# Second self attention: the last eight tiles' query, key and value products as three products of split factors

## The reference

```python
def _L1_attn_ref(x, ...):                       # x: (64, 32, 256), 16 heads, 16 wide, latent width 32
    qkv = x @ c_attn_w.T + c_attn_b
    q, k, v = jnp.split(qkv, 3, axis=2)         # into heads
    q_lat = q @ q2l_w.T + q2l_b
    k_lat = k @ kv2l_w.T + kv2l_b
    v_lat = v @ kv2l_w.T + kv2l_b
    q_lat = q_lat * cos + _rotate_half(q_lat) * sin
    k_lat = k_lat * cos + _rotate_half(k_lat) * sin
    q_for_k = q_lat @ wqk_w.T + wqk_b
    att = softmax(causal(q_for_k @ k_lat.T * L ** -0.5))
    y = (att @ v_lat) @ l2o_w.T + l2o_b
    return y @ cproj_w.T + cproj_b
...
x = x + _L1_attn_ref(_layernorm(x), ...)
x = x + tanh(((_layernorm(x) @ weight) @ aux1) @ aux2 + bias)
```

## Time and profile before

| | us |
|---|---|
| median of 3 runs | 2626.02 (2624.39 to 2628.48) |
| profiled execution | 2620.7 |
| its span, first to last instruction | 2618.9 |
| busy over the span: PE | 2439.4 (93%) |
| PEld | 1903.6 (73%) |
| DVE | 1696.1 (65%) |
| ACT | 1282.9 (49%) |
| POOL | 1475.7 (56%) |

### The profile page before, as it was taken

The page is one execution under the profiler, slowest core; times in us unless marked ns, Lnnn a source line. Parts: engine busy times, 40 slices in busy tenths (PEclk is TensorE's granted clock), DMA queues, the critical chain, the costliest instruction groups (busy, mean ns, idle before and its releaser), DMA issues. The chain is left out here.

```text
span 2618.9 us, 64377 instructions
## 1 busy us (share of the span) xinstructions
PE 2439.4 (93%) x24513; PEld 1903.6 (73%) x24513; DVE 1696.1 (65%) x3970; ACT 1282.9 (49%) x2972; POOL 1475.7 (56%) x1676
## 2 busy tenths in 40 slices
PE   6898999999999999998797999599999999998997
PEld 3457788888887878786465579478888888886665
DVE  5676868687868677774575844366556655653665
ACT  3565656565656565654342324254455445543443
POOL 6896767575767675764672245565456545332233
PEclk9999999999999999999897999799999999999998
DMA  4232212111111121110002459532234323210001
GB/s 166 113 140 79 61 36 50 34 46 39 41 40 46 34 50 34 46 32 8 30 5 94 142 165 314 185 119 76 67 95 103 75 68 94 71 45 15 3 4 35
DMA packets 223075, 190.04 MB, mean 73 GB/s; under 512 B 88705, under 2 KB 210514, under 8 KB 222770
## 3 DMA queue, kind: packets, MB, share of 16 engines
q1 hardware_dynamic: 206386, 151.19, 19.2%
q0 software_dynamic: 10080, 30.00, 4.5%
q10 hardware_dynamic: 6304, 4.72, 0.6%
HBM read 151.53 MB, written 34.31 MB: 71 GB/s over the span
## 5 line engine op out<-in xcount | busy, mean ns | idle before, releaser
L288 POOL TENSOR_TENSOR rk<-ss,neg_half 128x32 f32<-128x32 f32 x64 | 348.6, 5447 | 247.6 <-DVE ss L270 247.6
L1768 PE MATMUL banks<-rowsT,qk 128*128 128x257 f32 x1024 | 243.1, 380 | 0.9 <-ACT qk L1689 0.9
L321 ACT ACTIVATE ksq<-kT 128x512 f32<-128x512 f32 x256 | 161.1, 630 | 160.3 <-DVE kT L264 160.3
L264 DVE COPY kT<-banks 128x512 f32<-128x512 f32 x256 | 177.0, 692 | 60.7 <-PE banks L375 56.6
L375 PE MATMUL banks<-x_hi,wk_hi 128*128 128x256 f32 x1024 | 213.4, 289 | 1.1 <-DVE kT L264 1.0
L1768 PEld LDWEIGHTS banks<-rowsT,qk 128*128 128x128 f32 x1024 | 189.4, 190 | 27.5 <-ACT qk L1689 1.2
L375 PE MATMUL banks<-x_hi,wk_lo 128*128 128x256 f32 x1024 | 206.8, 284 | 0.0
L375 PE MATMUL banks<-x_lo,wk_hi 128*128 128x256 f32 x1024 | 205.6, 282 | 0.3 <-DVE x_lo L256 0.3
L1222 ACT ACTIVATE score<-score,ntop 128x289 f32<-128x289 f32 x256 | 135.4, 530 | 115.6 <-DVE ntop L1103 115.4
L1577 POOL DMA_INDIRECT parts<-scratch_expert,address x128 | 131.9, 1030 | 93.0 <-DVE residual L1475 45.9
L1606 POOL CAST r_hi<-diff 128x512 fp32r<-128x512 f32 x64 | 41.5, 648 | 249.9 <-PE banks L1794 249.1
(11 more groups left out here) (368 smaller groups left out, 6539.7 us busy)
## 6 DMA issues: line engine op xcount, KB each, us to landing
rowsT<-in_ctxT SPq DMA_DIRECT2D x64, 257.0 KB, 2.8
wgu<-in_expert_gu SPq DMA_DIRECT2D x64, 256.0 KB, 3.9
rows<-in_ctx SPq DMA_DIRECT2D x64, 256.0 KB, 3.2
raw<-in_ctx SPq DMA_DIRECT2D x61, 256.0 KB, 2.7
scratch_qT<-qT SPq DMA_DIRECT2D x16, 512.0 KB, 2.6
scratch_kT<-kT SPq DMA_DIRECT2D x16, 512.0 KB, 3.0
q<-scratch_qT SPq DMA_DIRECT2D x64, 128.0 KB
kT<-scratch_kT SPq DMA_DIRECT2D x64, 128.0 KB
```

The source lines that it names most:

```text
L264: nc.vector.tensor_copy(m.kT[:, k, 2 * i:2 * i + 2, 0:ROWS], banks[i % 2].rearrange("p (a r) -> p a r", a=2)).then_inc(s.kT, 1)
L288: nc.gpsimd.tensor_tensor(m.rk[:], m.ss[:], kit.neg_half[:, 0:KF * H], ALU.pow).then_inc(s.rk, 1)
L321: nc.scalar.activation(m.ksq[:, 2 * i:2 * i + 2, :], m.kT[:, k, 2 * i:2 * i + 2, 0:ROWS], ACT.Square).then_inc(s.ksq, 1)
L1768: mm = nc.tensor.matmul(score[h][:, c - h * HALF, 0:CTX], m.qk[:, f, j, c * BT:(c + 1) * BT, :].rearrange("p h q -> p (h q)"), m.rowsT[:, ...
```

## The change

In `sa1`, tiles 8 to 15 (`SPLIT` = 8): the transposed rows are written as a high part in fp32r (`x_hi`, by ScalarE, in place of `xlT`) and a low part (`x_lo`, a subtraction on VectorE out of the same bank). The weights are split once into `w_hi` (ScalarE copies) and `w_lo` (VectorE subtractions), in six pieces `CUTS` of 512, 512 and 256 columns for each half, one piece at the end of each of the steps -4 to 1. `product` then runs, after the bias, x_hi·w_hi, x_hi·w_lo and x_lo·w_hi for both halves: six fp32r products in place of two f32 ones. Tiles 0 to 7 and `sa0` keep theirs.

```diff
@@ buffers
+                            w_hi=([P, FC, QKV], F32R), w_lo=([P, FC, QKV], F32R), x_hi=([P, 2, FC, P], F32R), x_lo=([P, 2, FC, P], F32R))
+        SPLIT = 8 if rotary else NT
+        CUTS = [(f, slice(i * 512, min(i * 512 + 512, QKV))) for f in range(FC) for i in range(3)] if rotary else []
@@ VectorE
+                def weights_low(c):
+                    f, part = CUTS[c]
+                    dve.wait_ge(s.w_hi, c + 1)
+                    nc.vector.tensor_tensor(r.w_lo[:, f, part], w[:, f, part], r.w_hi[:, f, part].bitcast(F32), ALU.subtract).then_inc(s.w_lo, 1)
+
+                def rows_low(n):
+                    dve.wait_ge(s.xlT, n + 1)
+                    past(dve, s.qk_ps, (n - 1) * 2)
+                    past(dve, s.v_ps, n - 1)
+                    nc.vector.tensor_tensor(r.x_lo[:, n % 2].rearrange("p f t -> p (f t)"), kit.psum(0)[:, 0:D], r.x_hi[:, n % 2].rearrange("p f t -> p (f t)").bitcast(F32),
+                                            ALU.subtract).then_inc(s.x_lo, 1)
@@ VectorE, step
                     if has(3):
                         queries_keys(n + 3)
+                    if has(5) and n + 5 >= SPLIT:
+                        rows_low(n + 5)
                     if has(4):
                         if rotary:
                             cosines(n + 4)
                         else:
                             key_sums(n + 4)
+                    if rotary and 0 <= n + 4 < len(CUTS):
+                        weights_low(n + 4)
@@ ScalarE, rows_T
-                    nc.scalar.copy(m.xlT[:, n % 2].rearrange("p f t -> p (f t)"), kit.psum(0)[:, 0:D]).then_inc(s.xlT, 1)
+                    out = m.xlT if n < SPLIT else r.x_hi
+                    nc.scalar.copy(out[:, n % 2].rearrange("p f t -> p (f t)"), kit.psum(0)[:, 0:D]).then_inc(s.xlT, 1)
@@ ScalarE, step
                         inner(n + 4)
+                    if rotary and 0 <= n + 4 < len(CUTS):
+                        f, part = CUTS[n + 4]
+                        nc.scalar.copy(r.w_hi[:, f, part], w[:, f, part]).then_inc(s.w_hi, 1)
@@ TensorE
                     past(pe, s.xlT, n)
+                    past(pe, s.x_lo, n - SPLIT)
@@ TensorE, product
+                    if n >= SPLIT:
+                        for x, y in ((r.x_hi, r.w_hi), (r.x_hi, r.w_lo), (r.x_lo, r.w_hi)):
+                            for f in range(FC):
+                                mm = nc.tensor.matmul(out, x[:, n % 2, f, :], y[:, f, columns], start=False, stop=(x is r.x_lo and f == FC - 1))
+                        return mm
@@ TensorE, values
                     pe.wait_ge(s.xlT, n + 1)
+                    if n == SPLIT:
+                        pe.wait_ge(s.w_lo, len(CUTS))
+                    past(pe, s.x_lo, n - SPLIT + 1)
```

More of the change, by code:

```diff
@@ L2064, in self_attention @@
             r = kit.buffers(st, one=([P, P], BF16), causal=([P, HC, S], BF16),
-                            lat=([P, 2 * H, S], F32), turn=([P, 2 * H, S], F32), qrT=([P, 512], F32), qb=([P, 1], F32))
+                            lat=([P, 2 * H, S], F32), turn=([P, 2 * H, S], F32), qrT=([P, 512], F32), qb=([P, 1], F32),
+                            w_hi=([P, FC, QKV], F32R), w_lo=([P, FC, QKV], F32R), x_hi=([P, 2, FC, P], F32R), x_lo=([P, 2, FC, P], F32R))
             w = wm.w
@@ L2069, in self_attention @@
             w = wm.w
-        s = kit.sems(stage, "zero one masked gain qb xl xlT_ps xlT qk_ps v_ps sq raw v ss scaled rss lat cosed turned qk qT_ps kT_ps qrT qrT_ps qT kT s_ps "
+        s = kit.sems(stage, "zero one masked gain qb xl xlT_ps xlT qk_ps v_ps sq raw v ss scaled rss lat cosed turned qk qT_ps kT_ps qrT qrT_ps qT kT s_ps w_hi w_lo x_lo "
                      "top shift p mass rmass prob pT y_ps yT o_ps biased x_add passed")
```

## The result

The changed kernel takes 2635.2 us (median of 5), the kernel before beside it 2625.0: ratio 1.0046, 95% interval 1.0032 to 1.0059. It is 10 us slower where 0.4 was forecast, outside the range. The profiled execution took 2634.6, its span is 2631.6.

What follows compares the result with a forecast made beforehand. TensorE's order of work was taken to bound the step in the second self attention. Products -5.3, filling +5.7 and pauses 0 gave +0.4 us on the 2626.02 median: 2626.4 us, range 2621.0 to 2631.0.

Steps and rivals of the forecast that it cites:

- TensorE sets the step: Second self attention, tiles 8 to 15 projected: TensorE's order of work is the step's length; shortest step 10.84 us, then about 10.2.
- The products' price: Query and key banks 0.33 us shorter each, 5.3 us saved over eight tiles; the values' gain counted at nothing.
- The rows' low part: VectorE's subtraction of about 0.4 us per changed tile, ahead of the cosines, hidden in its wait for keys: costs nothing.
- The filling: Splitting the weights in steps -4 to 1: VectorE's subtractions meet GpSimd at SBUF and delay TensorE, 5.7 us together.
- The pauses in issue: TensorE's pauses in runs of small matmuls, over the eight steps: between -1.2 and +1.3 us, taken as 0.
- The tail: Attention of tiles 12 to 15 behind the last product: same instructions, so no change in time.
- The slower rival: Instruction supply bounds TensorE's step, longer pauses eat the products' gain, only the filling's 5.7 us is left: 2631.7; chance 0.10.
- point of decision: The slower rival decides once the pause of a step grows by 0.66 us, from 0.48 to 1.14.

Runs made afterwards that it cites:

- e_fill: The change with SPLIT = NT: weights split in six pieces but no tile uses them, all 16 keep f32 products; ratio 1.0034 to the kernel before.
- c_after: The changed kernel run again without an edit, on another chip; ratio 1.0036 to the kernel before.
- c_before: The kernel before run once more without an edit, as a control; ratio 0.9999.
- e_moved: The change with VectorE's low parts of the weights taken one step later, ahead of the cosines; ratio 1.0007 to the kernel before.
- e_one_input: The change with VectorE's weight subtractions replaced by same-size maxima with one SBUF input, low parts zero; ratio 1.0017 to the kernel before.
- m_mm128: e_moved with 64 one-column products (128 TensorE instructions) ahead of its first step; ratio 0.9983 to the kernel before, 2639.2 us against 2644.9.
- e_moved_2: e_moved run once more, unchanged; ratio 1.0001 to the kernel before, 2645.2 us against 2644.9.
- g_pad127: e_gain with 127 semaphore increments on TensorE ahead of the first step; ratio 1.0034 to the kernel before, stage 194.8 us.
- a_pad165: The change with 165 semaphore increments on TensorE ahead of the first step; ratio 1.0125 to the kernel before.
- b_mm128: The kernel before with 64 one-column products (128 TensorE instructions) ahead of the first step; ratio 1.0010 to the kernel before, 2648.3 us.
- e_gain: The change with split weights as constants set once, so no filling; ratio 1.0014 to the kernel before, stage 203.1 us.

## Why the prediction was wrong, point by point

- **TensorE sets the step**: right. Its floor came down to 10.2 us.
- **The products' price**: right. 1.61 us a bank for 1.93; forecast 0.33 less, measured 0.32. The values are shorter and the queries start no sooner: in the change the values' bias is at 2510.99 and the first product of the queries at 2512.00 (the record of their bias is missing), 1.01 us for 0.99 from bias to bias before. That they would wait for ScalarE's latents held.
- **The rows' low part**: right. No wait of TensorE for it in any profile, and in the change's VectorE waits for the keys' product in each of the eight changed steps.
- **The filling**: right in mechanism and in size. 5.5 us of TensorE's waits against 5.7; the subtraction at 1.37 against "about 1.4". Open: whether a pause behind one of these waits takes some of it up. In the change's first profile the pause of step 1 is gone and 3.3 us are lost; in e_fill and c_after the wait in step 1 is followed by the longest pause of the profile, and about 2 us more are lost than the waits hold.
- **The pauses in issue**: the step that failed. I put them between -1.2 and +1.3 us, took 0, and priced them by an average per step, from the first self attention. They are not an average. They stand where a block of instructions ends near the end of the mix, and the change moved these ends: among the eight steps, from 54 and 26 instructions ahead (steps 8 and 11) to 14 and 32 (7 and 10). The eight steps then have 8 x 10.21 = 81.7 us of work and 89.8 of length, 8.1 us of pause and slow clock, where before has 8 x 10.84 = 86.7 and 90.5, 3.8. That is +4.3 for the 0 taken, three times the upper end.
- **What a pause costs**: missing altogether. I counted pauses as idle time. In the change the clock goes to its lower level behind those of steps 7 and 10, and 1.63 and 1.36 us of pause become 3.2 and 3.1 us of step. In the kernel before, behind 1.74 us of pause, it stays at 1.00, so nothing in its trace showed it in the middle of this stage.
- **The tail**: wrong. "Same instructions, same time" is not so when their place in the blocks moves. The tail takes 31.6 us for 27.9, with a pause of 2.31 us at the output product of step 14 and the lower clock from there to the end of the stage. The pause is most of the 3.7 us; what the clock adds is not separated, since before runs its last 7 us at the lower level too, and c_before, all at 1.00, is only 0.6 us shorter. e_moved and e_one_input have this pause too, e_fill, in which TensorE's instructions are those of before, does not. TensorE in the change, then the busy times with the clock, from the change and from before:

```profile
2591.12 2.08 PE L2453 MATMUL banks<-wo,yT 128*128 128x256 f32 x4 [2.31 <-issue]
2593.12 1.49 PE L2443 MATMUL banks<-pT,v 32*32 32x32 f32 x123
2595.23 0.32 PE L2443 MATMUL banks<-pT,v 32*32 32x32 f32 x5 [0.62 <-issue]
2596.02 2.07 PE L2453 MATMUL banks<-wo,yT 128*128 128x256 f32 x4 [0.47 <-ACT yT L2321]
```

```profile
2591.10:2606.00 14.90, 9.43 (x269) 6.46 (x269) 6.31 (x18) 0.74 (x2) 1.77 (x4) 0.50 0.01 3
```

```profile
2586.00:2590.00 4.00, 3.06 (x89) 2.03 (x87) 1.00 (x4) 0.37 (x1) 0.00 (x0) 0.50 0.01 4
```

The sum as measured: filling 3.3 to 8 us (tile 5 in after, c_after and e_fill against before), products with their pauses -0.7, tail +3.7; about 6 to 11, and the medians show 10. The slower rival, instruction supply, named the cause: what the products save came back as longer pauses, 4.3 of 5.0 us in the eight steps. It got a chance of 0.10. Its size, 5.7 us (2631.7), was about half of the 10 measured, for it had no tail and no clock in it. Its point of decision was stated as a rate, and by rate it did not decide: m_mm128 has the same instructions in a shorter time and no pause above 0.9 us in the eight steps. It is a matter of place.

## What to carry to other kernels

Where TensorE runs hundreds of tiny matmuls in a microsecond or two, count its instructions: the pauses named "issue" repeat at places that can be computed from one profile (products left, times two, modulo 256, plus what a step adds). A change of a few instructions ahead of such runs moves them, and can cost or give as much as the change itself (m_mm128 against e_moved_2: 6 us); so compare with a few alignments before a verdict on a small gain. The places could be forecast, the lengths not always: step 6 of g_pad127, step 11 of a_pad165 and step 3 of b_mm128 came out other than expected. And an operation of VectorE with two SBUF inputs belongs where GpSimd is idle: one step later and ahead of a wait it was free here, at the end of the step it cost 5.5 us of TensorE's waits.

## What the runs showed of the hardware that I had not expected

- A pause of TensorE of 1.4 to 2.4 us in dense work can be followed by about 3 us at the lower clock: 0.57 behind 1.63 us in after, 0.52 behind 1.88 in e_gain, 0.63 behind 2.36 in c_after, but 1.00 behind 1.74 in before and behind 2.13 in step 11 of e_fill. The same pause at the same place, 1.88 us with 16 products to go in step 10, has the lower clock behind it in e_gain and the full one in e_moved:

```profile
2551.26:2554.50 3.24, 3.24 (x24) 1.97 (x24) 2.35 (x4) 1.06 (x2) 0.00 (x0) 0.52 0.00 0
```

```profile
2544.14:2547.38 3.24, 3.23 (x30) 2.28 (x30) 2.35 (x4) 1.50 (x4) 0.00 (x0) 1.00 0.00 0
```

  So a pause costs once or twice its length, and which it will be I can't tell from these runs.
- TensorE goes on 2.2 to 2.9 us after the start of the packet of its instruction queue, of which the packet itself takes 0.9 to 1.4 us (112 pauses).
- 127 semaphore increments on TensorE make its idle time ahead of the stage 24.4 us where it was 8.0, 0.13 us each beyond what the idle start hides, and 165 make it 30.2, 0.15 us for each one more. 64 one-column products cost nothing that the profile shows.
